# Own term, sum of four parts and clearing in the third and fourth pass of a graph kernel

## The reference

```
x = relu(x)
src, dst = edges followed by one loop (i, i) for each node
deg = segment_sum(1, dst);  dinv = rsqrt(max(deg, 1))
for _ in range(2):
    x = segment_sum(x[src] * dinv[src] * dinv[dst], dst)
```

## Time and profile before

| what | value |
|---|---|
| median of the runs shown | 11817.92 us |
| time of the profiled execution | 11816.44 us |
| its span, first to last instruction | 11814.7 us |
| busy: PE / DVE / ACT / POOL | 7462.7 / 6685.9 / 1846.8 / 8104.9 us |
| mean granted clock of TensorE | 0.79 |
| chain that ended last, by line | POOL L877 51%, PE L1083 6%, others 2% or less each |

### The profile page before, as it was taken

The page is one execution under the profiler, slowest core; times in us unless marked ns, Lnnn a source line. Parts: engine busy times, 40 slices in busy tenths (PEclk is TensorE's granted clock), DMA queues, the critical chain, the costliest instruction groups (busy, mean ns, idle before and its releaser), DMA issues.

```text
span 11814.7 us, 183469 instructions
## 1 busy us (share of the span) xinstructions
PE 7462.7 (63%) x56926; PEld 5697.7 (48%) x56926; DVE 6685.9 (57%) x18825; ACT 1846.8 (16%) x1630; POOL 8104.9 (69%) x8392
## 2 busy tenths in 40 slices
PE   7999897877666666667666666666666500321325
PEld 4675676767445554445445454555455400321324
DVE  9996212122666666666666666666666601553557
ACT  6996000000111111111111111111111000000000
POOL 6541776776677777757777775777777477777771
PEclk8998998999788888878888887878877755765767
DMA  3442665887100000010000001000000021221221
GB/s 110 139 146 101 192 194 169 293 261 256 17 13 13 13 13 13 13 16 13 13 13 13 13 13 16 13 13 13 13 13 13 10 44 32 62 53 40 62 51 38
DMA packets 654764, 750.92 MB, mean 64 GB/s; under 512 B 264009, under 2 KB 393499, under 8 KB 654165
## 3 DMA queue, kind: packets, MB, share of 16 engines
q10 hardware_dynamic: 202256, 401.00, 10.3%
q0 software_dynamic: 264960, 153.69, 8.5%
q1 hardware_dynamic: 187078, 190.14, 5.3%
HBM read 568.54 MB, written 175.70 MB: 63 GB/s over the span
## 4 chain that ended last, share of the span: by engine, by line
POOL 51%; issue 19%; PE 16%; DVE 4%; DMA 0%; DVEq 0%; ACT 0%; SPq 0%; POOLq 0%; ACTq 0%
POOL work L877 51%; PE ps L1083 6%; PE ps L1067 2%; PE ps L1068 1%; PE ps L1070 1%; PE ps L987 1%; PE ps L1117 1%; PE ps L1132 1%; PE ps L1066 1%; PE ps L1154 1%; PE ps L1237 1%; PE ps L1248 0%; PE ps L1213 0%; PE ps L1265 0%; DVE nodes L1729 0%
## 5 line engine op out<-in xcount | busy, mean ns | idle before, releaser
L877 POOL DMA_INDIRECT work<-tab_sp,nodes x4983 | 4716.0, 946 | 1721.4 <-issue 1517.0
L1132 PE MATMUL ps<-work 128*128 128x192 f32 x9984 | 2663.8, 411 | 1909.5 <-DVE work L1797 1847.6
L1132 PEld LDWEIGHTS ps<-work 128*128 128x128 f32 x9984 | 1986.0, 231 | 2485.7 <-issue 1438.0
L2050 DVE TENSOR_TENSOR work<-work,ps 128x192 f32 x4992 | 1745.9, 350 | 726.4 <-PE ps L1132 383.0
L877 POOL DMA_INDIRECT work<-tab_att,nodes x1661 | 1602.2, 965 | 629.6 <-issue 629.6
L1117 PE MATMUL ps<-work,wk 128*32 128x144 f32 x10080 | 1758.6, 327 | 2.3 <-DVE work L2050 2.3
L1797 DVE TENSOR_TENSOR work<-work,ps 128x512 f32<-128x512 f32 x1248 | 855.6, 686 | 1318.3 <-DMA work<-tab_sp,nodes 1292.1
L1450 ACT ACTIVATE work<-zero 128x2496 f32<-128x2496 f32 x318 | 725.4, 2282 | 5446.0 <-PE ps L1117 5441.4
L1117 PEld LDWEIGHTS ps<-work,wk 128*32 128x32 f32 x10080 | 1144.7, 124 | 558.0 <-issue 363.0
L2038 DVE TENSOR_TENSOR work<-work,ps 128x384 f32<-128x384 f32 x2496 | 1364.7, 547 | 0.0
L1882 DVE TENSOR_TENSOR big<-big,ps 32x12 f32 (+2 forms) x1600 | 248.3, 155 | 1262.0 <-PE ps L987 1046.4
(11 more groups left out here) (292 smaller groups left out, 8295.6 us busy)
## 6 DMA issues: line engine op xcount, KB each, us to landing
nodes<-counts_d ACTq DMA_DIRECT2D x648, 550.0 KB
counts_d<-nodes SPq DMA_DIRECT2D x50, 2475.0 KB
work<-tab_sp,nodes POOLq DMA_INDIRECT x4983, 2.4
work<-edge_rows SPq DMA_DIRECT2D x112, 320.0 KB
edge_rows<-work ACTq DMA_DIRECT2D x104, 320.0 KB, 2.2
work<-tab_att,nodes POOLq DMA_INDIRECT x1661
work<-tab_gcn,nodes POOLq DMA_INDIRECT x698
work<-tab_h,idx POOLq DMA_INDIRECT x509
```

The source lines that it names most:

```text
L877: pool.indirect_dma_start(out=rows(p, r)[:, t, 0:ROW[p]], out_offset=None, in_=TABLE[p], in_offset=bass.IndirectOffsetOnAxis(ap=place, axi ...
L1132: last = nc.tensor.matmul(moment_place(t), u0[:, s % 2, t % SUB, :], vb[:, t % AHEAD, :, :].rearrange("p k j -> p (k j)"), start=True, sto ...
L2050: v.tensor_tensor(to, to, got, ALU.add).then_inc(mom_added.sem, 1)
```

## The change

All of it is in close mode; the wide way keeps its turns.

- `turn("gin2")` and `turn("gcn1")` are no longer done on DVE, TensorE and ScalarE. `acc` begins with zeros, and the node phase adds `tb`, the own term, in the instruction that takes the sum out of PSUM.
- POOL clears all 128 partitions of a block in one instruction.
- In the node phase TensorE multiplies each tile of `acc`, as weights, by `ident4`, four identities of 32 below one another (128 x 32): the product is the sum of the four parts. DVE then has one addition and one product for a block instead of two reductions and a product.
- `load_counts` for gcn1 and gcn2 comes on ScalarE without a turn ahead of it; the wait for a free slot of the ring now names the last piece of the pass before that used the slot.
- SP waits for the end of gcn2's node phase before it loads `all_attr`, since `tb` is read until then.
- The signals of the turns get plans without gin2 and gcn1 for close mode.

```diff
@@ SP
-                        sp.wait_ge(parts_ready, len(UNITS))
+                        sp.wait_ge(out_done.sem, out_done.done(p, BLOCKS - 1))
@@ POOL, gathers
-                            pool.memset(acc[C:2 * C, cols], 0.0)
-                            pool.memset(acc[2 * C:3 * C, cols], 0.0)
-                            pool.memset(acc[3 * C:P, cols], 0.0).then_inc(acc_clear, 1)
+                            pool.memset(acc[:, cols], 0.0).then_inc(acc_clear, 1)
@@ TensorE, node phase
-                            w = P
-                            parts = ps[:, 2 * (b % 4) + j // SUB, (j % SUB) * w:(j % SUB + 1) * w]
-                            last = nc.tensor.transpose(parts, tile(w, b, j), ident[0:w, 0:w])
+                            last = nc.tensor.matmul(to(C), tile(P, b, j), ident4[:, :], start=True, stop=True)
@@ TensorE, rest
-                    if p != "gcn2":
+                    if p != "gcn2" and not close:
                         turn(p)
@@ ScalarE, load_counts
+                before = 0 if p == "gin2" else UNITS[LINEAR[LINEAR.index(p) - 1]] * NCH
...
-                    hold(act, "act", piece_used.sem, piece_used.done(p, c - PIECES))
+                    last_here = c - PIECES if c >= PIECES or not before else -1 - (before - 1 - r) % PIECES
+                    hold(act, "act", piece_used.sem, piece_used.done(p, last_here))
@@ ScalarE, rest
-                    turn(LINEAR[LINEAR.index(p) - 1])
                     if close:
                         load_counts(p)
+                    else:
+                        turn(LINEAR[LINEAR.index(p) - 1])
@@ DVE, node phase
-                        for t0, n in ((0, SUB), (SUB, BT - SUB)):
-                            parts = ps[:, 2 * (b % 4) + t0 // SUB, 0:n * P].rearrange("p (t q c) -> p t c q", q=QT, c=C)
-                            ins = v.tensor_reduce(dst[:, b * BT + t0:b * BT + t0 + n, :], parts, axis=AX.X, op=ALU.add)
-                        ins.then_inc(out_done.sem, 1)
+                        v.tensor_tensor(dst[:, tiles, :], got, tb[:, tiles, :], ALU.add).then_inc(out_done.sem, 1)
                         dve.wait_ge(out_done.sem, out_done.done(p, b))
                         link(v.tensor_tensor(dst[:, tiles, :], dst[:, tiles, :], over_features(scale[:, tiles], BT), ALU.mult))
@@ DVE, rest
-                turn("gin2")
+                if not close:
+                    turn("gin2")
...
-                turn("gcn1")
+                if not close:
+                    turn("gcn1")
```

More of the change, by code:

```diff
@@ L503, in build @@
         PROJ = ["sp1", "sp2", "sp3", "collect"]
-        tstaged = Signal(sem("tstaged"), {p: BLOCKS for p in TURNED[1:]})
-        turned_ps = Signal(sem("turned_ps"), {p: BLOCKS for p in TURNED}, lead=2)
-        turned = Signal(sem("turned"), {p: BLOCKS for p in TURNED}, lead=2)
+        close_turned = {p: BLOCKS for p in TURNED if p not in ("gin2", "gcn1")}
+        tstaged = Signal(sem("tstaged"), {p: BLOCKS for p in PROJ}, wide={p: BLOCKS for p in TURNED[1:]})
+        turned_ps = Signal(sem("turned_ps"), close_turned, lead=2, wide={p: BLOCKS for p in TURNED})
+        turned = Signal(sem("turned"), close_turned, lead=2, wide={p: BLOCKS for p in TURNED})
         proj_ps = Signal(sem("proj_ps"), {p: BLOCKS for p in PROJ}, lead=2)
```

## The result

The changed kernel takes 11839.15 us (median of 16 runs, 11829.54 to 11844.07) against 11818.31 for the kernel before beside it (16 runs, 11815.31 to 11823.24): ratio 1.0016, 95% interval 1.0009 to 1.0023, so 20.8 us slower. The forecast was 11837, with a range of 11801 to 11850.

What follows compares the result with a forecast made beforehand. The prediction took POOL's gathers to set the gcn1 and gcn2 passes, and TensorE to become the node phases' bound. Terms of +12.1 (gcn1) and +6.5 (gcn2) gave +18.6 us, hence 11837 us, range 11801 to 11850.

Steps and rivals of the forecast that it cites:

- turn that goes, by itself: Start of gcn1 and gcn2: TensorE may start 17 us earlier but then waits longer for gathers; gains nothing.
- splitting ahead of the gathers: Start of gcn1 and gcn2: splitting ends before the first gather, so three slow gathers become ordinary; -8.1 and -7.4 us.
- pieces that start earlier: Before gcn1: earlier count pieces share DMA engines with the table's store, delaying the gathers; +3.7 us, bounds 0 to 9.8.
- one clear before gcn2: Before gcn2: POOL no longer ends its clears after the table's store would allow a gather; -3.1 us.
- node phases: Node phases of gcn1 and gcn2: TensorE becomes the bound, mostly at half clock, 41.0 us each; +16.5 and +17.0 us.
- attribute load moved: Behind gcn2's node phase: the load is out of the way of sp1's table store; nothing, or up to 8 us.
- Rival 2: Between 1943.7 and 1960, before gcn1: the store gives way to the pieces, up to 9.8 us instead of 3.7; 20%.
- Rival 1: Node phases of gcn1 and gcn2: clock stays at or returns to 1.0, phases 22.1 us, total 11799 us; 11%.

Runs made afterwards that it cites:

- e5: The changed kernel with TensorE held in gcn1 and gcn2 until the first half of 16 gathers has landed; 11837.57 us, ratio 1.0016.
- e4: The kernel before with DVE splitting the table ahead of the turn in gcn1 and gcn2, turns kept; 11804.23 us, ratio 0.9988.
- e6: The changed kernel with ScalarE loading the count pieces of gcn1 only after gcn1's table is stored; 11836.64 us, ratio 1.0015.
- e11: The changed kernel, 32 moving columns kept, with POOL clearing a block in three instructions again; 11843.88 us.
- e10: The changed kernel with 128 moving columns in the gcn1 and gcn2 node phases and POOL clearing a block in three instructions again; 11814.35 us.
- e3: The changed kernel with 128 moving columns (ident4 read four times) in the node-phase products of gcn1 and gcn2; 11804.61 us, ratio 0.9988.
- e1: The kernel before with only the node-phase sum by ident4 products on TensorE, turns and three clears kept; 11851.77 us, ratio 1.0028.
- e7: The changed kernel with the old node phase (transposes, two reductions), then own term and product; 11814.03 us, ratio 0.9995.

## Why the prediction was right, point by point

From the end of the table's signal in gcn1 to the first gather of sp1 the profiled execution grew by 19.4 us (1036.60 to 1055.96), where +18.6 were forecast. Where two numbers stand, they are for gcn1 and gcn2. Each term, as measured:

| term | forecast | measured |
|---|---|---|
| turn that goes, by itself | 0 | 0 (e5: 24.5 us of late start cost nothing) |
| splitting ahead of the gathers | -8.1, -7.4 | -7.6, -7.2 |
| pieces that start earlier | +3.7 | +2.8 |
| one clear before gcn2 | -3.1 | -3.4 from signal to gather |
| node phases | +16.5, +17.0 | +15.6, +18.8 |
| attribute load moved | 0 | 0 |
| tails after the last gather | not forecast | -1.6, +1.9 |

*The turn that goes.* Right in size and mechanism: e4 has 14.8 us less in its gathers, where 15.5 were forecast for the splitting, with the turns in place, and e5 shows that TensorE's start is not on the path.

*The count pieces.* 2.8 came out where 3.7 was taken between bounds of 0 and 9.8, and e6 takes it back. Rival 2 asked for 4.7 or more.

*One clear.* The wait before gcn2's first gather went from POOL's clears to the store, as forecast, but the cause was misjudged and the agreement in size (-3.1 and -3.4) is luck: the single clear was priced at the old pace of the node phase. e11 shows that three clears would have kept up with 2.99 us a block as well; POOL was on time because TensorE was slow. With TensorE at full clock the single clear is worth 7.3 us from signal to gather (e10 against e3), 3.1 of them because two clears no longer meet casts, and 5.9 in the time.

*The node phase.* TensorE became the bound, and its clock halved. How long it stays at full was taken as 2.0 us; gcn1 had about 3 (0.92 over 3.8), gcn2 hardly any, and the two errors, -0.9 and +1.8, cancel in part. In e5, e6 and e11, which have the same products, the profiled phases last 40.3 to 42.5 us, so 41.0 lies within what single executions show. By an estimate from the rule of the Trainium skill ("TensorE: Matmul & The Clock Gate", section LDWEIGHTS) the phases would have been 22.1 us; evictions 2.99 us apart at 0.50 speak against it, as the rows of apply did. Rival 1 said 11799 for a clock that holds; e3, whose clock came back, measures 11804.6 with phases of 24.8 us in place of 22.1 (2 x 2.7 = 5.4 of the 5.6 between).

*The attribute load.* From sp1's table signal to its first gather it is 11.75 us, before 11.74, and the load is issued 24.6 us before that signal ends:

```profile
2965.23 0.35 SPq L762 DMA_DIRECT2D nodes<-in_attr_tile  x1
2989.93 6.59 SPq L670 DMA_DIRECT2D tab_sp<-xc  x4
```

*What was not forecast.* The tails of the two passes, from the last gather to the last sum, moved by -1.6 and +1.9 us, and cancel. That the sum came within 0.8 us of the forecast is in part luck: the terms were off by -0.9 to +1.8 and cancel too.

The profiled execution is a further 2.0 us late ahead of the change and 6.3 behind sp1's first gather (the gathers of sp1 to sp3 take 2.6 more, apply's products 39.7 us instead of 37.4). The code there is the same. From sp1's first gather to the end it is 8834.4 us in the profile before and 8840.7 after; e1 to e7, e10 and e11, with the same code from there on, lie between 8834.8 and 8839.2, with the changed code (e7 is the lowest) as with the old one. So this is spread, and the medians, 20.8 apart, hold little of it.

## What to carry to other kernels

Before an engine's instructions are made fewer by giving the work to TensorE, look in the trace for products of the same form and read the granted clock under them: here 32-column products ran at half clock to the end of their phase, and four times the columns ran faster. Removing work from an engine that waits later is worth what it moves, not what it took: ask which instruction comes earlier and what it no longer collides with. A saving that keeps one engine up with another is worth something only at the other's final pace, so price it after the terms that change that pace.

## What was not expected of the hardware

TensorE, continuously busy with products of a 128x128 f32 tile by a narrow f32 operand, fell to a granted clock of 0.50 with 32 columns in the node phases of gcn1, gcn2 and apply, and with 64 columns in both phases profiled; with 128 columns it fell to 0.67 over the first 5.1 us and came back to 1.0 without a pause. In gin2's node phase of the kernel before, 1.75 us of products of a 64x128 f32 tile by 32 columns alternate with 1.72 us of products of up to 512 columns; there the granted clock was 1.00 from 1880 to 1910. At full clock the 128 columns cost almost nothing over the 32: 1.57 us a block against 1.49. A clear on POOL and a cast on DVE that met in e4 took turns, so that they lasted 2.38 and 2.47 us instead of 0.84 and 1.79.
